# A four-layer graph network on one core: the three biases added by VectorE during the gathers, in place of TensorE's products at the layers' ends

## The chip, the core and the metric

The kernel runs on one NeuronCore of a Trainium2 chip. The metric is the device time of one execution in microseconds (us). Three runs of the kernel before took 8660.35, 8661.93 and 8672.08 us; their median, 8661.93 us, is its time.

## What is computed

Everything is float32. `x` has 12500 nodes of 32 features, and there are 200000 edges with a source, a destination, 32 attributes, a type of 86 and a weight; the edges come sorted by destination. Four layers follow, each with a residual:

```
h = relu(layernorm(x)); x = x + (h + segment_sum(relu(h[src] + edge_attr), dst)) @ W0.T + b0
h = relu(layernorm(x)); x = x + L1(h)
h = relu(layernorm(x)); x = x + relu(segment_sum(weight * h[src], dst) @ W2 + b2)
h = relu(layernorm(x)); x = x + segment_sum(h[src], dst) @ W3.T + b3
```

Layer 1 is a relational layer with 16 bases and attention. It adds, without a bias at its end, `relu(nei + curr)`, where `curr` is the row of one source (the node's last edge) times a self-loop weight.

## The kernel before

**Layout.** `x`, `h` and `t` lie in SBUF as 128 partitions x 98 blocks x 32 features, so 3136 columns. The sums over edges (`acc`) fill the first 3136 columns of PSUM: six banks of 512 columns and a seventh of which only 64 columns are used (BANKS = 7). The rest of PSUM's last bank holds small masks and, in its last 128 columns, `iota_ps`.

**A wide layer (0, 2 and 3).** The edges are cut into 1587 tiles of up to 128, four to a lot, so 397 lots: 49 rounds of eight (ROUNDS, RING) in a hardware loop and a remainder of five lots (REST) written out after it. For each lot POOL issues four gathers of 128 rows of the table of `h` in device memory (L511). It may run eight lots ahead of VectorE, whose buffers make the ring. VectorE makes one-hot matrices (L992) and spreads the gathered rows over four blocks of nodes (L1005 in layers 2 and 3; L1020, L1025 and L1030 in layer 0), and TensorE adds each tile to the sums (L1277). ScalarE copies the next indices (L586).

**A layer's end** is the time between the last gather of one layer and the first of the next. `linear` (L1305) goes over the seven banks. TensorE transposes the sums of a bank (L1300, four products with the identity), ScalarE copies them to SBUF (L613), and TensorE multiplies them by a block-diagonal weight (L1328, four products). The transposes of the next bank stand ahead of the products of this one in TensorE's queue. Ahead of the four products a fifth puts the bias into the bank: ones by `biasrow`, one partition deep and 512 columns wide (L1323), and the four accumulate on it. In layer 1, where there is no bias, a product of zeros stands there (L1320). In layers 2 and 3 ScalarE first copies the raw sums out of PSUM (L619); in layer 0 VectorE does that with `h` added (L1066).

**The residual and the norm.** VectorE runs `norm` in turns, one a bank, staggered: turn n holds the sum of squares of bank n-3 (L837), the centring of bank n-2 (L842), the sum of bank n-1 (L847) and then the residual of bank n (L1044, in layer 2 L1043, in layer 1 L1171), which waits for that bank's products. ScalarE squares each centred bank (L554). When all seven banks are through, a few short instructions on 98 columns (from L851 on) make the scale, seven more write `h` (L862), SP writes it to device memory, and POOL begins the next layer's gathers when all seven transfers have landed. After layer 3 there is no norm, and SP stores each bank of `x` when its residual is done (L443, the last one L445).

**Layer 1** first writes a table of products of all nodes. POOL meanwhile gathers 98 blocks of self-loop rows (L501), VectorE masks them (L1104) and `linear` with zeros follows. Then 104 rounds of 16 tiles run (STEPS_N / 16), with the gathers of POOL (L511 into `arena`), two long products of VectorE for each lot pair (L1138) and reductions (L1144). Its masks and coefficients overwrite `iota_ps`, which VectorE restores after the last round (L1167).

Of the kernel before, what the change touches and what calls it, by code (L numbers as in the profile page):

```python
# [82 lines left out]
def gnn(nc, x_in, src, dst, edge_attr, etype, weight, W0, b0, eps0, W1, wcomp, wself, A1, A1b, A2, A2b,  # L83
# [11 lines left out]
    with ctx:  # L95
# [5 lines left out]
        def sem(name):  # L101
            return ctx.enter_context(nc.semaphore(name))
# [53 lines left out]
        biasrow = sb("biasrow", [1, 3, D])  # L156
# [69 lines left out]
        iota_ps = ps[:, W7 + BANK - P:W7 + BANK]  # L226
        coef = ps[:, FEAT:FEAT + LOTS * HB * BASES].rearrange("p (h u b) -> p h u b", h=LOTS, u=HB)
# [40 lines left out]
        added = sem("residual_added")  # L268
        mean_ready = sem("mean_ready")
# [180 lines left out]
        def _(pool):  # L450
# [25 lines left out]
            for k, b in enumerate((b0, b2, b3)):  # L476
                pool.dma_start(biasrow[:, k, :], b.rearrange("(a f) -> a f", a=1)).then_inc(loaded, 16)
# [301 lines left out]
        def _(dve):  # L779
# [42 lines left out]
            def norm(l, residual):  # L822
# [9 lines left out]
                for turn in range(BANKS + 3):  # L832
                    b = turn - 3
# [100 lines left out]
            cp(wq[:, MSG + D:PROD], ps[:, W7 + 2 * P + D:W7 + 2 * P + 2 * D]).then_inc(wts_ready, 1)  # L934
# [72 lines left out]

            def wide_layer(l, body):

                with dve.Fori(0, ROUNDS) as i:  # L1010
                    body(i, RING)
                body(ROUNDS, REST)
# [24 lines left out]
            def linear_residual(q, relu):  # L1037

                def add(b):
                    w = columns(b)  # L1040
                    dve.wait_ge(lin_done, BANKS * q + b + 1)
                    if relu:
                        return nc.vector.scalar_tensor_tensor(xf[:, w], ps[:, w], 0.0, xf[:, w], ALU.max, ALU.add)  # L1043
                    return tt(xf[:, w], ps[:, w], xf[:, w], ALU.add)  # L1044
                return add

# [21 lines left out]
            norm(1, linear_residual(0, False))  # L1068
# [98 lines left out]
            step(cp(iota_ps, iota[:, :]))  # L1167
# [19 lines left out]
            norm(3, linear_residual(2, True))  # L1187
# [11 lines left out]
            last_add = linear_residual(3, False)  # L1199
# [5 lines left out]
        def _(pe):  # L1205
# [99 lines left out]
            def linear(q, w, bias):  # L1305

                for turn in range(BANKS + 1):
                    if turn < BANKS:
                        if bias is None:
                            pe.wait_ge(self_masked, turn + 1)  # L1310
                        else:
                            pe.wait_ge(t_ready, BANKS * (q if q < 2 else q - 1) + turn + 1)
                        transposes(selfrows.rearrange("p b f -> p (b f)") if bias is None else tf, turn)
# [3 lines left out]
                    n = min(BANK, FEAT - b * BANK)  # L1317
                    pe.wait_ge(hT_copied, BANKS * q + b + 1)
                    if bias is None:
# [14 lines left out]
            linear(0, 0, 0)  # L1334
# [31 lines left out]
            linear(1, 3, None)  # L1366
# [48 lines left out]
            linear(2, 1, 1)  # L1415
# [3 lines left out]
            linear(3, 2, 2)  # L1419
# [24 lines left out]
```

## Time and profile before

| | us |
|---|---|
| median of three runs | 8661.93 |
| lowest and highest | 8660.35, 8672.08 |
| the profiled execution, its own time | 8675.0 |
| its span in the profile | 8673.2 |
| busy: POOL | 6224.3 (72%) |
| busy: TensorE matmuls | 4674.7 (54%) |
| busy: VectorE | 4395.6 (51%) |
| busy: ScalarE | 2234.2 (26%) |

The profile records one execution. PE is TensorE's matmuls and PEld its weight loads, DVE is VectorE, ACT is ScalarE, POOL is GpSimd, SPq the queue that issues transfers. A line such as L1323 is a line of the kernel. TensorE's granted clock is given as a share of 2.4 GHz, so 0.50 is 1.2 GHz. Times of the timeline are us from the start of the span: start, duration, engine, line, operation; in brackets how long the engine had been idle before, and what ended that.

### The profile page before, as it was taken

The page shows a single profiled execution, that of the slowest core. Times are in us where ns is not written, and L with a number is a line of the kernel's source. Part 1 is how long each engine was busy: PE and PEld are TensorE (multiplying, and loading weights), DVE is VectorE, ACT ScalarE, POOL GpSimd, SP SyncE. Part 2 cuts the span into 40 slices and gives each one's busy share as a digit, 9 for nine tenths or more (in the row PEclk, how much of TensorE's full clock was granted, in tenths as well). Part 3 has the DMA queues.
Part 4 walks back from the last instruction along what each step waited for, and adds up shares of the span by engine and source line. Part 5 has one row for each costly group of instructions (what it writes and reads, how often), then busy time and mean ns, then how long its engine had stood idle before and what let it go on. Part 6 is the DMA issues. An engine that isn't in the chain of part 4 may idle for free. (4 is left out here: it accounts for less than half of the span.)

```text
span 8673.2 us, 104883 instructions
## 1 busy us (share of the span) xinstructions
PE 4674.7 (54%) x23835; PEld 4127.8 (48%) x23836; DVE 4395.6 (51%) x8833; ACT 2234.2 (26%) x5812; POOL 6224.3 (72%) x6577
## 2 busy tenths in 40 slices
PE   4555555555777777777774444444445444444444
PEld 3444444444677777777773333333333333333333
DVE  6555555555688888888884222222223222222222
ACT  1000000002688788888881000000000000000000
POOL 6777777776666666666665777777775777777776
PEclk6555555556555555555555555555555555555555
DMA  4111111113788888888881000000000000000001
GB/s 84 26 26 26 26 26 26 26 26 97 232 245 245 244 246 243 246 244 246 245 243 34 13 13 13 13 13 13 13 13 18 13 13 13 13 13 13 13 13 18
DMA packets 599594, 726.39 MB, mean 84 GB/s; under 512 B 339548, under 2 KB 433308, under 8 KB 596385
## 3 DMA queue, kind: packets, MB, share of 16 engines
q0 software_dynamic: 290064, 544.60, 24.1%
q1 hardware_dynamic: 309497, 181.39, 7.6%
q8 instruction: 16, 0.26, 0.0%
q14 instruction: 17, 0.14, 0.0%
HBM read 685.53 MB, written 40.64 MB: 84 GB/s over the span
## 5 line engine op out<-in xcount | busy, mean ns | idle before, releaser
L511 POOL DMA_INDIRECT lanes<-table,idx x4764 | 4522.7, 949 | 1546.7 <-issue 1451.4
L1277 PE MATMUL ps<-arena 128*128 128x128 f32 x9528 | 2718.5, 458 | 3232.5 <-DVE arena L1005 2337.4
L1277 PEld LDWEIGHTS ps<-arena 128*128 128x128 f32 x9528 | 2267.9, 328 | 3644.8 <-issue 3570.0
L511 POOL DMA_INDIRECT arena<-table,idx x1664 | 1581.3, 950 | 756.7 <-issue 485.1
L1005 DVE TENSOR_TENSOR arena<-lanes,ps 128x512 f32<-128x512 f32 x794 | 545.7, 687 | 2858.5 <-DMA lanes<-table,idx 2858.5
L586 ACT COPY idx<-tabs 128x4 int32 (+1 forms) x1191 | 228.3, 193 | 5727.9 <-DMA lanes<-table,idx 5723.1
L992 DVE TENSOR_TENSOR arena<-ps,node 128x512 f32<-128x512 f32 (+1 forms) x1588 | 1048.3, 680 | 0.0
L1269 PE MATMUL ps<-lanes 128*128 128x32 f32 x3328 | 752.2, 402 | 485.1 <-issue 281.4
L1269 PEld LDWEIGHTS ps<-lanes 128*128 128x128 f32 x3328 | 725.4, 330 | 511.8 <-issue 511.8
L1377 PE MATMUL ps<-t,arena 128*128 x3328 | 955.0, 402 | 0.0
L1377 PEld LDWEIGHTS ps<-t,arena 128*128 128x128 f32 x3328 | 860.3, 318 | 0.1
L1375 PEld LDWEIGHTS ps<-relparts,arena 128*128 128x128 bf16 x4992 | 593.9, 171 | 167.9 <-ACT arena L710 156.9
L1020 DVE TENSOR_TENSOR lanes<-lanes 128x128 f32<-128x128 f32 x397 | 118.8, 299 | 980.6 <-DMA lanes<-table,idx 971.6
L1375 PE MATMUL ps<-relparts,arena 128*128 128x48 bf16 x4992 | 510.3, 219 | 140.2 <-ACT arena L710 140.2
L743 ACT ACTIVATE arena<-iota,tabs 128x128 f32<-128x128 f32 x1664 | 531.6, 392 | 0.0
L1138 DVE TENSOR_TENSOR arena<-arena,ps 128x2048 f32<-128x2048 f32 x208 | 475.6, 2286 | 7.1
L1138 DVE TENSOR_TENSOR tT<-arena,ps 128x2048 f32<-128x2048 f32 x208 | 474.1, 2279 | 0.0
L1144 DVE TENSOR_REDUCE lanes<-tT 128x128 f32<-128x2048 f32 x208 | 473.3, 2275 | 0.0
L1144 DVE TENSOR_REDUCE lanes<-arena 128x128 f32<-128x2048 f32 x208 | 473.3, 2275 | 0.0
L722 ACT ACTIVATE arena<-arena,part 128x1024 f32<-128x1024 bf16 x416 | 472.5, 1136 | 0.3
L1030 DVE SCALAR_TENSOR_TENSOR arena<-lanes,ps 128x128 f32<-128x128 f32 x1588 | 344.5, 277 | 0.0
L1280 PE MATMUL ps<-lastrow,arena 128*128 128x8 bf16 x1588 | 339.8, 214 | 0.0
(201 smaller groups left out, 2908.9 us busy)
## 6 DMA issues: line engine op xcount, KB each, us to landing
arena<-step_rows SPq DMA_DIRECT2D x416, 256.0 KB, 4.6
lanes<-table,idx POOLq DMA_INDIRECT x4764, 2.4
arena<-table,idx POOLq DMA_INDIRECT x1664, 4.1
table<-arena SPq DMA_DIRECT2D x24, 1088.0 KB, 6.0
lanes<-in_edge_attr SPq DMA_DIRECT2D x384, 64.0 KB
table<-h SPq DMA_DIRECT2D x18, 256.0 KB, 2.4
edge_rows<-arena SPq DMA_DIRECT2D x1, 2496.0 KB, 8.4
lanes<-self_loop_table,selfi POOLq DMA_INDIRECT x98, 2.4
```

The lines of the kernel that those rows point to most:

```text
L511: pool.indirect_dma_start(out=into, out_offset=None, in_=tableD[l], in_offset=bass.IndirectOffsetOnAxis(ap=index, axis=0)).then_inc(there, 16)
L722: nc.scalar.activation(off[:, :, :, :], rowb[:, k], ACT.Abs, scale=-1.0, bias=part[:, 0:1]).then_inc(off_ready[k], 1)
L743: last = nc.scalar.activation(away[:, u, :], iota[:, :], ACT.Abs, scale=-1.0, bias=tabs[:, DLOC, bass.ds(i * BODY + (k * HB + u), 1)])
L992: tt(to[:, k], iota_ps.unsqueeze(1).to_broadcast([P, HB, P]), node[:, bass.ds(i * ROUND + (EXN + k * HB), HB)].unsqueeze(2).to_broadcast([ ...
L1005: tt(wmsg[:, k], rows_[:, k].unsqueeze(2).to_broadcast([P, HB, WB, D]), factors[:, k].unsqueeze(3).to_broadcast([P, HB, WB, D]), ALU.mult) ...
L1030: last = nc.vector.scalar_tensor_tensor(wmsg[:, k, u], total[:, k % LOTS, u].unsqueeze(1).to_broadcast([P, WB, D]), 0.0, mask[:, k, u].uns ...
L1138: tt(prods[k % 2][:, :, :, :], g1[:, k, :, 0:MSG].rearrange("p u (o b) -> p u o b", o=D), coef[:, k].unsqueeze(2).to_broadcast([P, HB, D, ...
L1144: nc.vector.reduce_sum(msg[:, k], prods[k % 2][:, :, :, :], AX.X).then_inc(msg_ready[k], 1)
L1269: last = mm(ps[:, bass.ds(w[u], D)], onehot[:, k, u, :], msg[:, k, u], start=False, stop=True, skip_group_check=True)
L1277: last = mm(ps[:, bass.ds(w[u], WB * D)], onehotw[:, k, u, :], wmsg[:, k, u].rearrange("p w f -> p (w f)"), start=False, stop=True, skip_g ...
L1375: mm(ps7[:, u, :], relT[:, k, u, :], relparts[:, part_, :], start=(part_ == 0), stop=False, skip_group_check=True)
L1377: last = mm(ps7[:, u, BASES:YC], nodeT[:, k, u, :], yf[:, bass.ds(w[u], D)], start=False, stop=True, skip_group_check=True)
```

## The change

VectorE adds the bias to `x` in one instruction of 3136 columns between the hardware loop and the five last lots of a wide layer, while POOL gathers. The operand that is repeated over the 98 blocks is `bias_ps`, 96 columns of PSUM that VectorE fills in the prologue and again after layer 1. In layer 2 the bias stands inside the relu, so there the sum goes to `h`, which is free by then: `h = x + b2`. At the end `h` takes up the products, and `x` becomes the larger of `h` and `x`, because x + relu(y) = max(x + y, x). Thus a bank takes two instructions there, and the first of them stands at the head of its turn. TensorE no longer multiplies ones or zeros; the first of the four products of a bank opens the accumulation itself. The bias vectors are loaded into all 128 partitions.

```diff
@@ buffers
-        biasrow = sb("biasrow", [1, 3, D])
+        biasrow = sb("biasrow", [P, 3, D])
+        bias_ps = ps[:, W7 + BANK - P - 3 * D:W7 + BANK - P].rearrange("p (k f) -> p k f", k=3)
+        summed = sem("sums_and_bias_added")
@@ POOL, prologue
-                pool.dma_start(biasrow[:, k, :], b.rearrange("(a f) -> a f", a=1)).then_inc(loaded, 16)
+                pool.dma_start(biasrow[:, k, :], b.partition_broadcast(P)).then_inc(loaded, 16)
@@ VectorE, norm
-            def norm(l, residual):
+            def norm(l, residual, sums=None):
...
                 for turn in range(BANKS + 3):
+                    if sums and turn < BANKS:
+                        sums(turn).then_inc(summed, 1)
@@ VectorE, prologue
-            cp(wq[:, MSG + D:PROD], ps[:, W7 + 2 * P + D:W7 + 2 * P + 2 * D]).then_inc(wts_ready, 1)
+            step(cp(wq[:, MSG + D:PROD], ps[:, W7 + 2 * P + D:W7 + 2 * P + 2 * D]))
+            cp(bias_ps, biasrow[:, :, :]).then_inc(wts_ready, 1)
@@ VectorE, wide layers
+            def add_bias(to, k):
+
+                step(tt(to[:, :, :], x[:, :, :], bias_ps[:, k].unsqueeze(1).to_broadcast([P, BLOCKS, D]), ALU.add))
+
             def wide_layer(l, body):
 
                 with dve.Fori(0, ROUNDS) as i:
                     body(i, RING)
+                if l == 2:
+                    dve.wait_ge(table_out[2], BANKS * 16)
+                add_bias(h if l == 2 else x, TURN[l])
                 body(ROUNDS, REST)
@@ VectorE, residuals
-            def linear_residual(q, relu):
+            def linear_residual(q):
...
-                    if relu:
-                        return nc.vector.scalar_tensor_tensor(xf[:, w], ps[:, w], 0.0, xf[:, w], ALU.max, ALU.add)
                     return tt(xf[:, w], ps[:, w], xf[:, w], ALU.add)
...
+            def sums_of_2(b):
+
+                w = columns(b)
+                dve.wait_ge(lin_done, BANKS * 2 + b + 1)
+                return tt(hf[:, w], ps[:, w], hf[:, w], ALU.add)
+
+            def relu_residual(b):
+
+                w = columns(b)
+                dve.wait_ge(summed, b + 1)
+                return tt(xf[:, w], hf[:, w], xf[:, w], ALU.max)
@@ VectorE, end of layer 1
-            step(cp(iota_ps, iota[:, :]))
+            cp(iota_ps, iota[:, :])
+            step(cp(bias_ps, biasrow[:, :, :]))
@@ VectorE, end of layer 2
-            norm(3, linear_residual(2, True))
+            norm(3, relu_residual, sums_of_2)
@@ TensorE, linear
-                    if bias is None:
-                        mm(ps[:, b * BANK:(b + 1) * BANK], zeros[0:1, 0:P], zeros[0:1, :], start=True, stop=False,
-                           skip_group_check=True)
-                    else:
-                        mm(ps[:, b * BANK:b * BANK + n], ones[0:1, :],
-                           biasrow[:, bias, :].unsqueeze(1).to_broadcast([1, n // D, D]), start=True, stop=False,
-                           skip_group_check=True)
...
                         last = mm(ps[:, g * P:g * P + m], tT[0:m, g * P:(g + 1) * P], wdiag[0:m, w, 0:m],
-                                  start=False, stop=True, skip_group_check=True)
+                                  start=(g == 4 * b), stop=True, skip_group_check=True)
```

## Rows read from the trace of the kernel before

**Rows 1.** Groups by line: busy us, mean ns of one, idle before and its releasers.

```profile
L511 POOL DMA_INDIRECT lanes<-table,idx x4764 | 4522.7, 949 | 1546.7 <-issue 1451.4 <-DMA table<-h 95.3
...
L511 POOL DMA_INDIRECT arena<-table,idx x1664 | 1581.3, 950 | 756.7 <-issue 485.1 <-DVE arena L1138 270.1 <-DVE tT L1138 1.5
```

**Rows 2.** Timeline of the end of layer 3.

```profile
8639.09 1.97 PE L1300 MATMUL ps<-ident,t 128*128 128x128 f32 x8 [0.75 <-ACT t L619]
...
8640.99 2.07 PE L1323 MATMUL ps<-biasrow,ones 1*128 1x512 f32 x2
...
8642.99 2.08 PE L1328 MATMUL ps<-wdiag,tT 128*128 128x128 f32 x8
...
8645.85 2.07 PE L1323 MATMUL ps<-biasrow,ones 1*128 1x512 f32 x2
...
8668.66 0.69 PE L1323 MATMUL ps<-biasrow,ones 1*128 1x64 f32 x2
...
8670.00 0.23 DVE L1044 TENSOR_TENSOR x<-ps,x 128x64 f32<-128x64 f32 x1 [0.54 <-PE ps L1328]
```

**Rows 3.** Stretches: window, length, busy by engine, granted PE clock, DMA share, GB/s.

```profile
8650.00:8660.00 10.00, 10.00 (x31) 6.33 (x30) 1.66 (x3) 1.77 (x4) 0.00 (x0) 0.50 0.33 52
2077.80:2078.40 0.60, 0.60 (x2) 0.00 (x0) 0.06 (x1) 0.09 (x1) 0.00 (x0) 0.88 0.00 0
6627.80:6628.40 0.60, 0.60 (x3) 0.30 (x2) 0.60 (x2) 0.54 (x1) 0.00 (x0) 0.91 0.00 0
```

**Rows 4.** Timeline of the end of layer 0.

```profile
2070.44 1.97 PE L1300 MATMUL ps<-ident,t 128*128 128x128 f32 x8 [1.68 <-DVE t L1066]
...
2076.45 0.69 DVE L1044 TENSOR_TENSOR x<-ps,x 128x512 f32<-128x512 f32 x1 [2.59 <-PE ps L1328]
...
2082.70 1.12 PE L1323 MATMUL ps<-biasrow,ones 1*128 1x512 f32 x2
...
2085.28 1.12 PE L1323 MATMUL ps<-biasrow,ones 1*128 1x512 f32 x2
...
2095.86 0.21 DVE L851 TENSOR_SCALAR small<-small 128x98 f32<-128x98 f32 x1
```

**Rows 5.** Timeline of the end of layer 1.

```profile
4589.22 0.29 DVE L1167 COPY ps<-iota 128x128 f32<-128x128 f32 x1 [3.67 <-PE ps L1269]
4589.55 0.69 DVE L1171 SCALAR_TENSOR_TENSOR x<-ps,x 128x512 f32<-128x512 f32 x1
...
4605.76 0.21 DVE L851 TENSOR_SCALAR small<-small 128x98 f32<-128x98 f32 x1
```

**Rows 6.** Timeline of the end of layer 2.

```profile
6606.41 1.97 PE L1300 MATMUL ps<-ident,t 128*128 128x128 f32 x8 [0.68 <-ACT t L619]
...
6612.43 0.69 DVE L1043 SCALAR_TENSOR_TENSOR x<-ps,x 128x512 f32<-128x512 f32 x1 [8.89 <-PE ps L1328]
...
6639.02 0.21 DVE L851 TENSOR_SCALAR small<-small 128x98 f32<-128x98 f32 x1
```

**Rows 7.** Timeline of the start of layer 1's rounds.

```profile
2232.61 0.23 DVE L1104 TENSOR_TENSOR lanes<-lanes,has_edge 128x64 f32<-128x64 f32 x1 [3.20 <-DMA lanes<-self_loop_table,selfi]
...
2234.84 0.26 ACT L613 COPY tT<-ps 64x128 f32<-64x128 f32 x1 [3.63 <-PE ps L1300]
```

**Rows 8.** Groups by line, VectorE's long product in layer 1.

```profile
L1138 DVE TENSOR_TENSOR arena<-arena,ps 128x2048 f32<-128x2048 f32 x208 | 475.6, 2286 | 7.1
```

**Rows 9.** Timeline of VectorE in the first of layer 0's five last lots.

```profile
2042.21 0.29 DVE L1020 TENSOR_TENSOR lanes<-lanes 128x128 f32<-128x128 f32 x1 [2.56 <-DMA lanes<-table,idx]
```

**Rows 10.** Groups by line in the stretch 65 to 78 us.

```profile
L511 POOL DMA_INDIRECT lanes<-table,idx x8 | 12.5, 1564 | 2.4 <-issue 2.4
...
L966 DVE TENSOR_SCALAR arena<-arena 128x1697 int32<-128x1697 int32 x1 | 1.1, 1120 | 0.0
```

**Rows 11.** Stretches of layer 1, VectorE's line L1138 alone, eleven of 200 us.

```profile
3100.00:3300.00 200.00, 78.13 (x35) 0.50 0.81 243
...
sum 2200.00, DVE 876.51; mean DVE 79.68
```

More of the change, by code:

```diff
@@ L226, in gnn @@
         iota_ps = ps[:, W7 + BANK - P:W7 + BANK]
+        bias_ps = ps[:, W7 + BANK - P - 3 * D:W7 + BANK - P].rearrange("p (k f) -> p k f", k=3)
+        assert 2 * ROUND * WB + 3 * D + P <= BANK
         coef = ps[:, FEAT:FEAT + LOTS * HB * BASES].rearrange("p (h u b) -> p h u b", h=LOTS, u=HB)
@@ L1067, in _ @@
                                                ).then_inc(t_ready, 1)
-            norm(1, linear_residual(0, False))
+            norm(1, linear_residual(0))
             yf = y[:, :, :].rearrange("p b f -> p (b f)")
@@ L1198, in _ @@
             wide_layer(3, body3)
-            last_add = linear_residual(3, False)
+            last_add = linear_residual(3)
             for b in range(BANKS):
@@ L1303, in _, with linear @@
             tf, hf = (v[:, :, :].rearrange("p b f -> p (b f)") for v in (t, h))
-            def linear(q, w, bias):
+            def linear(q, w, of_self):
                 for turn in range(BANKS + 1):
                     if turn < BANKS:
-                        if bias is None:
+                        if of_self:
                             pe.wait_ge(self_masked, turn + 1)
@@ L1312, in linear @@
                             pe.wait_ge(t_ready, BANKS * (q if q < 2 else q - 1) + turn + 1)
-                        transposes(selfrows.rearrange("p b f -> p (b f)") if bias is None else tf, turn)
+                        transposes(selfrows.rearrange("p b f -> p (b f)") if of_self else tf, turn)
                     b = turn - 1
@@ L1316, in linear @@
                         continue
-                    n = min(BANK, FEAT - b * BANK)
                     pe.wait_ge(hT_copied, BANKS * q + b + 1)
-                    if bias is None:
-                        mm(ps[:, b * BANK:(b + 1) * BANK], zeros[0:1, 0:P], zeros[0:1, :], start=True, stop=False,
-                           skip_group_check=True)
-                    else:
-                        mm(ps[:, b * BANK:b * BANK + n], ones[0:1, :],
-                           biasrow[:, bias, :].unsqueeze(1).to_broadcast([1, n // D, D]), start=True, stop=False,
-                           skip_group_check=True)
                     for g in range(4 * b, min(4 * b + 4, GROUPS)):
@@ L1333, in _ @@
             scatters(0)
-            linear(0, 0, 0)
+            linear(0, 0, False)
             def transpose_parts(g):
@@ L1365, in _ @@
             pe.wait_ge(p1_biased, BLOCKS)
-            linear(1, 3, None)
+            linear(1, 3, True)
             def edge_terms(i, k, w, n):
@@ L1414, in _ @@
             scatters(2)
-            linear(2, 1, 1)
+            linear(2, 1, False)
             pe.wait_ge(added, 4 * BANKS)
@@ L1418, in _ @@
             scatters(3)
-            linear(3, 2, 2)
+            linear(3, 2, False)
 _INS = ['x', 'src', 'dst', 'edge_attr_32', 'edge_type_86', 'edge_weight', 'L0_gnn_W', 'L0_gnn_b', 'L0_gnn_eps',
```

## The prediction

> **What bounds the kernel now.** I read the page's busy times first, then the groups by line, then the timeline of the ends, because the change touches little else. In the wide layers POOL is the bound. A gather takes 0.95 us and 0.30 us of issue (1451.4 / 4764) follow, so one starts every 1.25 us, and POOL's idle time before these gathers has no other entry but 95.3 us in which it waited for a table [rows 1]. Work of VectorE in those stretches costs nothing as long as it fits; work taken out of a layer's end, where POOL stands still, counts in full. In layer 1 POOL waits 270.1 us for VectorE's products, so its rounds are a circle of VectorE, POOL and transfers.
>
> In layer 3's end TensorE is the bound: it is busy for 10.00 of 10.00 us [rows 3]. A bank there takes 8645.85 - 8640.99 = 4.86 us, of which the bias product is 8642.99 - 8640.99 = 2.00 us [rows 2]. These are rows at a granted clock of 0.50, the lower level. In layer 0's end the clock rose at about 2077.9 us [rows 3], some 7.4 us after the first transposes, and from there on a bank takes 2085.28 - 2082.70 = 2.58 us, with 1.1 us of bias in it [rows 4].
>
> VectorE sets the floor of the other ends. Layer 1's end has no products to wait for: from the first residual to the scale it takes 4605.76 - 4589.55 = 16.2 us [rows 5]. Four instructions of a full bank start some 0.6 us apart, so a turn is 2.4 us. The same stretch takes 2095.86 - 2076.45 = 19.4 us in layer 0 [rows 4] and 6639.02 - 6612.43 = 26.6 us in layer 2 [rows 6].
>
> **The change, part by part.** All is measured against the profiled execution, 8675.0 us; the median of the runs is 13.1 us below it, and I carry the difference over unchanged.
>
> *Clock of the new ends.* Without the bias a bank costs TensorE 4.86 - 2.00 = 2.86 us at the lower level and 2.58 - 1.1 = 1.5 us at the upper. Which level is granted no row can show, since no end before was free of these products. What the engine did before each of the two rises was the same: four products and four transposes without a break, the last things ahead of a bias product. In layer 3's end each such stretch is broken by a one-partition product after 2.9 us, and the clock stayed at 0.50 for 30 us although TensorE was never idle [rows 2, 3]. In the new ends nothing breaks the stretch. So I take the clock to rise in each of them as late as it did in layer 0, 7.4 us after the first transposes, and hold both extremes for the range.
>
> The Trainium skill (TensorE: Matmul & The Clock Gate, Part 1) says that the throttled level is the default and that sustained activity releases it. Taken for busy time alone this disagrees with the trace, where an always busy TensorE was left at 1.2 GHz; for the new ends it would give the upper level, as I forecast.
>
> *Layer 0's end.* The first residual comes 2.0 us earlier, at 2074.45. If it never waited, the scale would follow 16.2 us later, at 2090.7: 5.2 us gained. But VectorE is ready for the second residual 1.3 us after the first (0.7 + 0.6), and the second bank's products come 2.86 us after the first's, at the lower clock: a wait of 1.55 us. The third is then ready about in time. **3.7 us** gained. At the lower level throughout, further waits of 1.06 us (2.86 - 1.8) and three of 0.46 us (2.86 - 2.4) leave 1.2 us. Ends: 1.2 and 5.2 us.
>
> *Layer 1's start.* The zero products go too. POOL's self-loop gathers hide most of them, but the transposes of the last bank stood behind one. Their input is ready at 2232.61 + 0.23 = 2232.84, and ScalarE's copy starts at 2234.84 [rows 7]; with 0.5 us for the few transposes of the narrow bank (eight take 1.97 us [rows 2]) it can start at 2233.4. ScalarE makes the first selectors right behind that copy, and the rounds start with these. **1.4 us** gained. It carries through, if the circle keeps its rhythm; between 0 and 1.5 us.
>
> *Layer 1's end.* One more copy, 96 columns behind 128. The first with its wait takes 4589.55 - 4589.22 = 0.33 us [rows 5], and the second overlaps it in part: **0.2 us lost** (0.1 to 0.33).
>
> *Layer 2's end.* Again the first products come 2.0 us earlier, at 6610.4. VectorE has 16.2 us of norm as in layer 1 and now seven sums on top, 6 x 0.6 + 0.3 = 3.9 us, so 20.1 us and the scale at 6630.5 instead of 6639.02: 8.5 us. A wait of 1.55 us before the second sum leaves **6.9 us**; at the lower level throughout, waits of 1.06 and 0.5 us more leave 5.3 us. From the fourth bank on a turn of five instructions (3.0 us) is longer than a bank of TensorE at either level (2.86 us), so VectorE becomes the bound here. That the sum stands at the head of its turn, ahead of three instructions of the norm, costs nothing in that case, because it doesn't wait.
>
> *Layer 3's end.* From 8639.09 to 8670.00 are 30.9 us [rows 2]. Six bias products of 2.00 us and the narrow one (0.69 us at most) go: 12.7 us, if the clock stays low. If it rises after 7.4 us, 18.2 - 7.4 = 10.8 us of lower-level work are left and shrink by 1.5 / 2.86 to 5.7 us: 4.9 us more, 17.6 in all. VectorE has one 0.7 us instruction a bank, and ScalarE two copies; both fit. The stores are next: at 0.33 of the transfer engines over 10 us, or two banks, one bank's store takes 1.6 us [rows 3], a little more than the 1.5 us in which banks now come. I take off 0.6 us: **17.0 us**. Ends: 12.7 and 18.6.
>
> *The adds under the gathers.* The nearest row is VectorE's product of 2048 columns with an operand in PSUM, 2.29 us [rows 8]; 3136 columns are 3.5 us. Between lots VectorE is idle for 2.56 us even in layer 0 [rows 9], so the first of the five last lots is 0.9 us late and the second has caught up; layers 2 and 3 have more room. POOL may run eight lots ahead and sees nothing. Gone is that cover only if the add stops POOL itself, a rival below. **0**.
>
> *The prologue.* A copy and a wait on VectorE (0.3 us) and three slightly larger loads of POOL's queue. VectorE's first lot waits for other data anyway, and POOL waits for a transfer behind its loads. **0**, at most 0.3 us lost.
>
> Sum: 3.7 + 1.4 - 0.2 + 6.9 + 17.0 = 28.8 us. 8675.0 becomes 8646.2, and the median 8661.9 - 28.8 = **8633 us**. Of the sum, 8 to 9 us rest on the clock.
>
> **Rivals.** A measurement of this kernel tells a change of 0.2% (17.3 us) from none: below 8644.6 us is faster, above 8679.3 slower.
>
> *The clock stays low in the new ends.* For it speaks that it did so for 30 us in layer 3; against it, that what kept the stretches short is what is removed. Then 1.2 + 1.4 - 0.2 + 5.3 + 12.7 = 20.4 us: 8641.5 us. Chance 0.22.
>
> *The adds stop POOL.* In the prologue eight gathers took 1564 ns each while VectorE ran integer instructions of 1697 columns at about 0.6 ns a column [rows 10], against 949 ns [rows 1]. So VectorE can hold up a gather, by about its own duration. Three adds of 3.5 us would cost 10.5 us: 8643.6 us. Against it: the 2286 ns products of layer 1 are of the add's kind, one operand in PSUM and about 1.1 ns a column, and the gathers beside them keep 950 ns [rows 1, 8]. Chance 0.06.
>
> The Trainium skill (GPSIMD Engine Reference, section 8, Key points) names contention with instructions in a two-port mode or with two inputs in SBUF. By that the add, with one input in PSUM, is free, and the sum would stay as it is.
>
> *Slower: the rounds of layer 1 settle into another rhythm.* They start with transfers, VectorE and POOL offset otherwise. In the slices of 200 us VectorE's products hold 78.13 us in the poorest and 79.68 us in the mean [rows 11]; poorest throughout would be 1.9% of the 2357 us between the last mask and the copy at the end (2232.61 to 4589.22 [rows 5, 7]), 45 us longer: 8678 us. It decides from 0.28 us a round on (28.8 / 104), below which the kernel is still faster. Against it: the slices differ by no more than the products that an edge cuts off, over 2000 us, so the circle looks stable. Chance 0.04.
>
> *The circle absorbs the early start* or small waits take as much: up to 5 us less than forecast, 8638 us; it is inside the forecast's own range.
>
> **How the numbers follow.** The forecast, with the clock up in some or all of the ends, has 0.65; its own range is 8627 (all upper ends, 34 us, and a little) to 8638. The rivals hold 0.32, and 0.03 is left for what I don't see. The range reaches down to 8623, since the runs before differ by up to 12 us and their median may stand some us off, and up to 8646, which takes in the low clock and stopped gathers. Faster: 0.65, most of the low clock's 0.22 and half of the stopped gathers' 0.06, together 0.86. Slower by over 0.2%: 0.03. Within: 0.11.
>
> **What would show it.** In the profile after: no L1323 or L1320 groups; a bank of layer 3's end 2.9 us and later 1.5 us long, with a granted clock of 1.00 before the last banks; layer 2's end with VectorE without a gap from the fourth turn on and the scale 20 to 22 us after the first sum; three adds of 3.4 to 3.5 us with gathers of 0.95 us beside them; the first selector distances 1.4 us sooner after the last mask. It is wrong if the granted clock stays at 0.50 in all ends, if a gather beside an add is longer, or if the stretch of layer 1's rounds changes by more than 2 us.

## The result and the profile after

On the chip of the prediction's runs the changed kernel takes 8642.41 us (median of 9 runs, 8637.83 to 8646.37). The kernel before takes 8668.71 us there (median of 9, 8660.35 to 8673.08). The ratio is 0.997, 95% interval [0.9962, 0.9978], so the change saves 26.3 us (19 to 33 us).

The two profiled executions are 34.0 us apart: 8675.0 and 8640.96 us, spans 8673.2 and 8639.1 us. The profiled run of before lies 6.3 us above its median and the one of after 1.5 us below; 34.0 - 6.3 - 1.5 = 26.2 us, which is what the medians say. The ledger below is of the profiles and so adds up to 34 us; some 8 us of that belong to these two executions and not to the change, and in which rows they lie one profile of each kernel can't show.

Groups of instructions of the kernel after, by line (busy us, mean ns of one, idle before and its releasers). L514 is the gather, L1344 the products and L1324 the transposes of `linear`; before they were L511, L1328 and L1300.

```profile
L514 POOL DMA_INDIRECT lanes<-table,idx x4764 | 4522.6, 949 | 1538.4 <-issue 1450.3 <-DMA table<-h 86.9 <-DVE lanes L1033 0.9
...
L514 POOL DMA_INDIRECT arena<-table,idx x1664 | 1581.1, 950 | 753.8 <-issue 486.0 <-DVE arena L1161 266.8 <-DVE tT L1161 0.9
...
L1344 PE MATMUL ps<-wdiag,tT 128*128 128x128 f32 (+1 forms) x200 | 34.4, 325 | 6.3 <-ACT tT L616 6.1
```

Beside [rows 1] the gathers and their issue are unchanged, and POOL waits 8.4 us less for tables. Those 8.4 us are not all of the gain, since the idle time before the first gather into `arena` and the end after the last gather don't count there. The groups of the bias products and of `linear`'s zero products are gone.

**Layer 0's end.** Timeline of after (start, duration, engine, line, idle before):

```profile
2070.44 1.97 PE L1324 MATMUL ps<-ident,t 128*128 128x128 f32 x8 [1.68 <-DVE t L1089]
...
2074.32 1.06 PE L1344 MATMUL ps<-wdiag,tT 128*128 128x128 f32 x8
...
2075.65 1.06 PE L1344 MATMUL ps<-wdiag,tT 128*128 128x128 f32 x8
```
VectorE in the same end:

```profile
2074.09 0.69 DVE L1055 TENSOR_TENSOR x<-ps,x 128x512 f32<-128x512 f32 x1 [0.22 <-PE ps L1344]
...
2075.41 0.69 DVE L1055 TENSOR_TENSOR x<-ps,x 128x512 f32<-128x512 f32 x1
...
2090.31 0.21 DVE L856 TENSOR_SCALAR small<-small 128x98 f32<-128x98 f32 x1
```

Four products and four transposes take 1.33 us (2075.65 - 2074.32) from the second bank on, and the second residual doesn't wait. Beside [rows 4] the first residual is 2.36 us earlier and the scale 5.55 us.

The granted clock of the three ends stands in the stretches of after (window, length, busy by engine, granted clock, DMA share, GB/s). Layer 0's end:

```profile
2073.00:2074.50 1.50, 1.50 (x13) 1.50 (x12) 1.28 (x4) 0.03 (x1) 0.00 (x0) 0.79 0.04 11
2074.50:2076.00 1.50, 1.50 (x16) 1.50 (x16) 1.47 (x3) 0.73 (x2) 0.00 (x0) 1.00 0.00 0
```
Layer 2's end:

```profile
6603.00:6604.00 1.00, 1.00 (x10) 1.00 (x9) 0.97 (x2) 0.54 (x2) 0.00 (x0) 0.94 0.00 0
```
Layer 3's end:

```profile
8627.00:8628.00 1.00, 1.00 (x10) 1.00 (x9) 0.57 (x1) 0.43 (x1) 0.00 (x0) 0.88 0.00 0
8628.00:8630.00 2.00, 2.00 (x20) 2.00 (x20) 0.90 (x2) 1.72 (x4) 0.00 (x0) 1.00 0.83 131
8630.00:8633.00 3.00, 3.00 (x29) 3.00 (x28) 1.72 (x3) 1.55 (x4) 0.00 (x0) 1.00 1.18 183
8633.00:8636.00 3.00, 0.78 (x6) 0.52 (x5) 0.96 (x3) 0.00 (x0) 0.00 (x0) 1.00 1.60 177
```

The clock rises 3.2, 4.3 and 4.3 us after the first transposes of the ends of layers 0, 2 and 3. In the kernel before it rose 7.5 us and 21.5 us after them in layers 0 and 2, and not at all in layer 3's [rows 2, 3].

**Layer 2's end**, VectorE's timeline of after; L1062 adds the products to `h`, L1068 is the new residual:

```profile
6602.76 0.69 DVE L1062 TENSOR_TENSOR h<-ps,h 128x512 f32<-128x512 f32 x1 [6.78 <-PE ps L1344]
6603.48 0.69 DVE L1068 TENSOR_TENSOR x<-h,x 128x512 f32<-128x512 f32 x1
6604.35 0.69 DVE L1062 TENSOR_TENSOR h<-ps,h 128x512 f32<-128x512 f32 x1 [0.17 <-PE ps L1344]
...
6611.53 0.68 DVE L1062 TENSOR_TENSOR h<-ps,h 128x512 f32<-128x512 f32 x1
...
6614.52 0.69 DVE L1062 TENSOR_TENSOR h<-ps,h 128x512 f32<-128x512 f32 x1
...
6622.98 0.21 DVE L856 TENSOR_SCALAR small<-small 128x98 f32<-128x98 f32 x1
```

A turn is 2.99 us, five instructions, and the only wait for products is 0.17 us. From the first sum to the scale are 20.2 us, where before 26.6 us went by [rows 6]. VectorE is the bound.

**Layer 3's end**, timeline of after; L446 and L448 issue the stores:

```profile
8622.97 1.97 PE L1324 MATMUL ps<-ident,t 128*128 128x128 f32 x8 [0.75 <-ACT t L622]
...
8627.60 8.85 SPq L446 DMA_DIRECT2D out_nodes<-x  x7
...
8628.70 1.06 PE L1344 MATMUL ps<-wdiag,tT 128*128 128x128 f32 x8
...
8630.03 1.06 PE L1344 MATMUL ps<-wdiag,tT 128*128 128x128 f32 x8
...
8633.45 0.82 DVE L1055 TENSOR_TENSOR x<-ps,x 128x512 f32<-128x512 f32 x2 [0.31 <-PE ps L1344]
8636.49 0.42 SPq L448 DMA_DIRECT2D out_nodes<-x  x1
```

A bank takes 1.33 us in place of 4.86 us [rows 2]. The residuals are through at 8634.27, but the last store is issued at 8636.49: the stores run at 131 to 183 GB/s, against 52 in the row of before [rows 3], and end last. (Their DMA share of 1.60 adds up transfers that are under way at the same time, so it can pass 1.)

**Layer 1**, timeline of its start in after:

```profile
2227.06 0.23 DVE L1127 TENSOR_TENSOR lanes<-lanes,has_edge 128x64 f32<-128x64 f32 x1 [1.85 <-DMA lanes<-self_loop_table,selfi]
...
2228.34 0.26 ACT L616 COPY tT<-ps 64x128 f32<-64x128 f32 x1 [1.33 <-PE ps L1324]
```
And of its end:

```profile
4581.30 0.29 DVE L1190 COPY ps<-iota 128x128 f32<-128x128 f32 x1 [3.70 <-PE ps L1293]
4581.51 0.25 DVE L1191 COPY ps<-biasrow 128x96 f32<-128x96 f32 x1
...
4598.00 0.21 DVE L856 TENSOR_SCALAR small<-small 128x98 f32<-128x98 f32 x1
```

The ledger, forecast beside measured:

| stretch | forecast us gained | measured |
|---|---|---|
| up to layer 0's end, adds and prologue | 0 | 0.0 |
| layer 0's end | 3.7 | 5.55 |
| layer 1's start (last mask to copy: 2.23, now 1.28) | 1.4 | 0.95 |
| layer 1's rounds (copy to copy: 2354.38, now 2352.96) | 0 | 1.4 |
| layer 1's end | -0.2 | -0.2 |
| wide loops of layers 2 and 3 | 0 | -0.1 |
| layer 2's end | 6.9 | 8.5 |
| layer 3's end | 17.0 | 17.9 |
| sum | 28.8 | 34.0 |

### The profile page after: what moved, and what is told of

Read it like the earlier page. It is cut to its first block and busy times, and to the rows that moved or that the text cites. A ratio compares the mean times of both kernels' runs of the same rounds, so it can differ in the third digit from the quotient of the medians.

```text
span 8639.1 us, 104786 instructions
## 1 busy us (share of the span) xinstructions
PE 4614.4 (53%) x23779; PEld 4105.4 (48%) x23780; DVE 4408.8 (51%) x8845; ACT 2233.6 (26%) x5812; POOL 6224.5 (72%) x6577
## 5 line engine op out<-in xcount | busy, mean ns | idle before, releaser
L514 POOL DMA_INDIRECT lanes<-table,idx x4764 | 4522.6, 949 | 1538.4 <-issue 1450.3
L514 POOL DMA_INDIRECT arena<-table,idx x1664 | 1581.1, 950 | 753.8 <-issue 486.0
```

What stands on the lines that cost most here:

```text
L514: pool.indirect_dma_start(out=into, out_offset=None, in_=tableD[l], in_offset=bass.IndirectOffsetOnAxis(ap=index, axis=0)).then_inc(there, 16)
```

## Experiments

Two causes were to be told apart: what made the clock rise (the missing one-partition products, or chance), and whether the adds and VectorE's new instructions cost what the sum says. The twelve runs fell on three other chips, A, B and C. There the kernel before takes 10295 to 10404 us, most of it because its wide loops are slower. The groups of 1000 us of layer 3 in the kernel before, on the first chip:

```profile
L511 POOL DMA_INDIRECT lanes<-table,idx x801 | 757.2, 945 | 244.2 <-issue 244.2
```
The same on chip C (before_b):

```profile
L511 POOL DMA_INDIRECT lanes<-table,idx x692 | 653.2, 944 | 356.6 <-issue 205.3 <-DVE arena L1005 149.4 <-ACT idx L586 1.9
...
L987 DVE TENSOR_TENSOR ps<-ps,tabs 128x16 f32<-128x16 f32 x179 | 31.7, 177 | 756.3 <-remote 657.2 <-issue 94.1 <-PE ps L1277 4.5
```

A gather is as long, but POOL now waits for VectorE, and VectorE for something that the profile doesn't name. The mean granted clock over these 1000 us is 0.58, against 0.50 on the first chip. What makes these chips slower stays open. The ends of the layers, where the change works, are made of the same instructions with the same durations, so kernels are compared by their ends and by ratios on one chip. Two kernels that are the same up to layer 0's end (after_again and l3zero_b) reach it 8.5 us apart there, and layer 1's rounds, which are the same in all four kernels on chip B, take 2908.4 to 2915.0 us in their profiles. So medians tell less than the ends do.

The ends of all profiles in us, from the timelines and the record of the granted clock: when the clock rises after the first transposes of layer 0's end; layers 0's and 2's ends from the first transposes to the scale; layer 3's to the end of the span.

| kernel, chip | clock rises | layer 0 | layer 2 | layer 3 | ratio to before, 95% |
|---|---|---|---|---|---|
| before, first | 7.5 | 25.4 | 32.6 | 34.1 | |
| after, first | 3.2 | 19.9 | 24.1 | 16.2 | 0.997 [0.9962, 0.9978] |
| before_again, A | 12.4 | 27.7 | 22.2 | 21.5 | |
| deep, A | 4.1 | 22.4 | 20.9 | 18.4 | 0.9989 [0.9981, 0.9998] |
| l3zero, A | 4.6 | 20.5 | 22.5 | 23.7 | 0.9982 [0.9973, 0.999] |
| onesum, A | 4.0 | 20.3 | 18.8 | 14.8 | 0.9967 [0.9955, 0.9979] |
| after_again, B | 5.4 | 20.9 | 22.5 | 14.8 | 0.9978 [0.9969, 0.9987] |
| l3zero_b, B | 5.8 | 21.1 | 22.5 | 21.2 | 0.9984 [0.9975, 0.9993] |
| threeadds, B | 4.5 | 20.5 | 22.5 | 14.8 | 0.9985 [0.9976, 0.9993] |
| poolboth, B | 3.6 | 22.4 | 23.1 | 14.8 | 0.9986 [0.9977, 0.9995] |
| before_b, C | 21.7 | 32.6 | 22.2 | 20.6 | |
| deep_b, C | 4.3 | 22.5 | 20.9 | 18.4 | 0.9979 [0.997, 0.9988] |
| allzero, C | 16.7 | 29.8 | 25.8 | 29.2 | 0.9998 [0.999, 1.0007] |
| pooladd, C | 4.4 | 20.5 | 21.8 | 14.8 | 0.9981 [0.9972, 0.9989] |

### The kernel before, twice

No edit.

> The kernel before, unchanged, for a second profile of it. The runs of before lie between 8660 and 8673 us. If the place at which the granted clock rises in the layers' ends makes that spread, the two profiles differ in the lengths of the ends (layer 2's 26.6 us from the first residual to the scale, layer 3's 30.9 us from the first transposes to the last residual) and agree elsewhere to 1 us. The rival, that the rounds of layer 1 or the gathers make it, has the ends equal to 0.5 us and another stretch longer or shorter by several.

> The kernel before once more: when the granted clock rises in its layers' ends. If its one-partition products keep the clock low, it rises 7 us or more after the first transposes of layer 0's end, as in the profile of before (7.4 us) and on the second kind of chip (12.5 us), where the changed kernel and the others without such products had 3.2 to 5.8 us. Rival (the moment is chance): anywhere between 3 and 13 us.

Measured: 10398.98 and 10289.78 us. Stretches of layer 0's end in before_b:

```profile
2421.00:2436.00 15.00, 15.00 (x46) 9.50 (x45) 6.01 (x10) 2.92 (x5) 0.00 (x0) 0.50 0.00 0
2436.00:2440.50 4.50, 4.50 (x20) 2.46 (x19) 3.82 (x7) 1.48 (x3) 0.00 (x0) 0.88 0.00 0
```
And nearly all of layer 3's:

```profile
10267.40:10282.00 14.60, 14.41 (x77) 9.00 (x77) 3.46 (x5) 6.16 (x13) 0.00 (x0) 1.00 0.46 73
```

The clock rose 12.4 and 21.7 us after the first transposes in layer 0's end, later than the 7.5 us of the first chip, and until then TensorE was busy without a gap. That is before_b's theory (7 us or more); its rival, 3 to 13 us by chance, is passed by far. What before_again was to find, where the first chip's spread of 13 us comes from, stays open, because it ran on another chip. In the ends of layers 2 and 3 the clock was already up when they began, since 4.8 to 7.2 us before the first transposes: there a bank takes 2.58 us, and the ends are 10 and 13 us shorter than on the first chip. So the clock's part of the gain differs from chip to chip.

### Bias products 128 partitions deep

The kernel before, with the same number of products of the same columns:

```diff
-                        mm(ps[:, b * BANK:b * BANK + n], ones[0:1, :],
-                           biasrow[:, bias, :].unsqueeze(1).to_broadcast([1, n // D, D]), start=True, stop=False,
+                        mm(ps[:, b * BANK:b * BANK + n], deep[:, :],
+                           biasrow[:, bias, :].unsqueeze(1).to_broadcast([P, n // D, D]), start=True, stop=False,
```

`deep` holds 1/128 everywhere and `biasrow` the bias in each partition.

> The kernel before with its bias products 128 partitions deep instead of one: weights of 1/128 everywhere and the bias vector in all partitions, so the same 512 columns and the same sums. My theory, that one-partition products kept the clock down: the clock rises within 4 to 8 us of an end's first transposes; layer 3's end shrinks from 30.9 to about 20 us, layer 2's from 26.6 to about 18, layer 0's by 1 to 3, in all 17 to 23 us less than before. The rival, that the clock follows the amount of TensorE's work or chance and not the depth of these products: granted clock 0.50 through layer 3's end as before, and a time within 4 us of before.

> The kernel before with its bias products 128 partitions deep (all ones/128 against the bias in all 128 partitions): as many products, columns and cycles as before. Theory (it is the one-partition form that keeps the clock low): the clock rises within 6 us of the first transposes in layer 0's end, and on a chip where before's layer 3 stays at 0.50 it rises there too, so that this end takes some 20 us in place of 30.9 and the kernel is 10 us or more faster than before. Rival (form is of no account): rise and ends as in the kernel before, time within 4 us of it.

Measured: 10392.24 us (11.4 us less than before) and 10279.41 us (16.0 us less). TensorE in layer 0's end of deep_b:

```profile
2416.32 1.97 PE L1302 MATMUL ps<-ident,t 128*128 128x128 f32 x8 [1.68 <-DVE t L1068]
2418.12 2.07 PE L1325 MATMUL ps<-biasrow,deep 128*128 128x512 f32 x2
...
2421.60 1.02 PE L1325 MATMUL ps<-biasrow,deep 128*128 128x512 f32 x2
2422.46 1.05 PE L1330 MATMUL ps<-wdiag,tT 128*128 128x128 f32 x8
```

A stretch of it:

```profile
2420.60:2421.40 0.80, 0.80 (x10) 0.80 (x9) 0.04 (x1) 0.00 (x0) 0.00 (x0) 1.00 0.00 0
```

At the lower level the deep product has the flat one's 2.07 us [rows 2], and yet the clock rises after 4.1 and 4.3 us in place of 12.4 and 21.7. Order, number and columns of TensorE's instructions are those of before; what differs is the depth of one in five, with the values that go with it, and a little of its time: from its start to the next row it takes 1.86 us (2419.98 - 2418.12) where the flat one takes 2.00 [rows 2]. So it is the one-partition form that keeps the clock low. Whether by its depth or by a short pause beside it that the records don't show, of which the 0.14 us may be a sign, stays open. As to the times, deep's forecast of 17 to 23 us less than before missed, with 11.4, and deep_b's of 10 us or more was met, with 16.0. Both had counted on ends of layers 2 and 3 that stay at the lower level, and on these chips they don't. The ends of layers 2 and 3 are 1.3 and 2 to 3 us shorter too, although the clock was up in both kernels: from its start to the next row a deep product takes 0.86 us at the upper level (2422.46 - 2421.60), a flat one 1.05 us in before_b.

### One-partition products of zeros put back

The changed kernel, for the end of layer 3 alone (l3zero, l3zero_b) or for those of layers 0, 2 and 3 (allzero, `q != 1`):

```diff
+                    if q == 3:
+                        n = min(BANK, FEAT - b * BANK)
+                        mm(ps[:, b * BANK:b * BANK + n], zeros[0:1, 0:P], zeros[0:1, 0:n], start=True, stop=False,
+                           skip_group_check=True)
...
-                                  start=(g == 4 * b), stop=True, skip_group_check=True)
+                                  start=(q != 3 and g == 4 * b), stop=True, skip_group_check=True)
```

> The changed kernel with one product of zeros, one partition deep, put back ahead of the four of each bank in layer 3's end alone, as wide as the bias product was. My theory: the clock stays at 0.50 for most of that end and its banks take about 4.9 us again, so 17 to 19 us more than the changed kernel. The rival, that the clock now rises anyway and only the products' own time counts: banks of 2.4 to 2.6 us, the clock at 1.00 after some 5 us, and 6 to 9 us more.

> The changed kernel with one one-partition product a bank (its left operand zero) ahead of the products of layer 3's end alone. Theory (broken stretches keep the clock low): on a chip on which the kernel before shows a granted clock of 0.50 all through layer 3's end, this end is again at 0.50 and as long as before, 30.9 us from the first transposes to the last residual, so that 16 to 19 us of the change's gain are gone and 8 to 15 are left. Rival (the clock rises with busy time, whatever the form of the products): it rises here some 4 us after the first transposes as in the changed kernel, the products added cost 1.1 us a bank, and the end is about 8 us longer than the changed kernel's, 22 us in all.

> The changed kernel with a one-partition product of zeros ahead of each bank's products in the ends of layers 0, 2 and 3: TensorE's work is as before, the rest is the changed kernel's. Theory (broken stretches keep the clock low): in layer 0's end the clock rises 7 us or more after the first transposes, and that end's gain (5 to 7 us) is gone; in layer 3's end 2.0 us a bank are back at the lower clock, 1.05 us at the upper; in layer 2's end VectorE is the bound at either level, so it is lengthened by no more than its first two banks. In all 14 to 24 us slower than the changed kernel, no faster than before by more than 10 us. Rival (the clock rises as in the changed kernel, 3 to 6 us after the transposes): the ends of layers 0 and 3 are 4 and 8 us longer, 12 us in all.

Measured: 10386.57, 10282.75 and 10297.12 us. Stretches of allzero in layer 0's end:

```profile
2426.00:2436.00 10.00, 10.00 (x31) 6.22 (x29) 3.54 (x6) 1.70 (x3) 0.00 (x0) 0.50 0.00 0
2436.50:2441.00 4.50, 4.50 (x25) 2.78 (x25) 3.88 (x7) 2.14 (x4) 0.00 (x0) 1.00 0.00 0
```
And in layer 3's end of allzero:

```profile
10267.30:10270.00 2.70, 2.52 (x13) 1.45 (x14) 0.00 (x0) 2.44 (x5) 0.00 (x0) 1.00 0.00 0
10270.00:10287.00 17.00, 17.00 (x55) 11.17 (x54) 2.77 (x4) 3.01 (x8) 0.00 (x0) 0.50 0.29 46
10287.00:10290.00 3.00, 3.00 (x13) 1.51 (x13) 0.69 (x1) 0.71 (x2) 0.00 (x0) 0.98 0.56 87
```
The low stretch of l3zero in the same end:

```profile
10357.30:10364.00 6.70, 6.70 (x24) 4.54 (x23) 1.38 (x2) 1.07 (x2) 0.00 (x0) 0.50 0.25 39
```
And l3zero_b's end, in two stretches:

```profile
10255.60:10270.60 15.00, 14.81 (x79) 9.09 (x78) 3.46 (x5) 5.94 (x13) 0.00 (x0) 1.00 0.44 70
10270.70:10273.00 2.30, 2.30 (x11) 1.96 (x9) 0.69 (x1) 0.00 (x0) 0.00 (x0) 0.50 0.72 114
```

With allzero the whole gain is gone: 0.9998 of before, and by the ratios, each of which is good to some 9 us, 20 us more than the changed kernel on its chip. In layer 0's end the clock rises late again, 16.7 us after the first transposes, and in layer 3's it even falls from the upper level and stays at 0.50 for 17 us while TensorE is never idle. The same happened in l3zero for 6.8 us, but in l3zero_b only 15.3 us after the first transposes, so that there the product cost little more than its own 1.05 us a bank: 21.2 against 14.8 us. Falls of the clock under a TensorE that had been busy without a gap for 13 us or more occur in five profiles, one each in the three of before, in l3zero_b and in allzero (23.3 us after the first transposes), and each time in an end with one-partition products. In the ends without them the clock fell only where TensorE had gaps. (The early falls, 2.8 us into the end in allzero and 2.9 in l3zero, come after 0.75 and 0.18 us in which TensorE waited.) So one-partition products can hold the clock down, and these profiles suggest that they let it fall, too; when it happens varies from run to run.

The forecasts: allzero's theory holds in the time (14 to 24 us) and in layer 0's end. For layer 3 alone the theory missed: l3zero's end is 8.9 us longer than onesum's on the same chip, not 17 to 19, and l3zero_b's 6.4 us longer than after_again's, near the rivals' 6 to 9 and 8 us. An end of 30.9 us, as on the first chip, came in neither run. Here the end began with the clock up, so the chip that l3zero_b's theory asks for was not met. Layer 2's end is 25.8 us in allzero, 3.6 us longer than in before: with the clock up and the products still there, VectorE's second instruction a bank is a pure cost.

The Trainium skill (TensorE: Matmul & The Clock Gate, Part 1) has the gate follow how busy TensorE has been. The row of 15.00 busy us in 15.00 at 0.50 shows that the busy time of the records is not enough; the measurement decides.

### One instruction a bank in layer 2

The changed kernel with the fused residual of before in layer 2. Nothing adds b2, so this output lacks it.

```diff
-            norm(3, relu_residual, sums_of_2)
+            def one_residual(b):
+
+                w = columns(b)
+                dve.wait_ge(lin_done, BANKS * 2 + b + 1)
+                return nc.vector.scalar_tensor_tensor(xf[:, w], ps[:, w], 0.0, xf[:, w], ALU.max, ALU.add)
+
+            norm(3, one_residual)
```

> The changed kernel, but layer 2's end has one instruction a bank again (the larger of products and zero, added to x); the bias of layer 2 is left out of the result, while its add under the gathers still runs. My theory, that VectorE bounds this end at both levels: the seven sums are gone and the stretch from the first of VectorE's residuals to the scale falls from 20.2 to 16.2 to 16.8 us, 3.5 to 4 us less in all. The rival, that TensorE or ScalarE's copies and squares come next: under 1.5 us less.

Measured: 10372.45 us, 0.9967 of before. Layer 2's end is 18.8 us against 22.5 us in l3zero on the same chip: 3.7 us for six sums of a full bank and a narrow one, which is the prediction's 3.9 us. The other ends are the changed kernel's.

### The changed kernel, and three wide adds in place of one

```diff
-                add_bias(h if l == 2 else x, TURN[l])
+                to = h if l == 2 else x
+                add_bias(to, TURN[l])
+                for op in (ALU.subtract, ALU.add):
+                    step(tt(to[:, :, :], to[:, :, :], bias_ps[:, TURN[l]].unsqueeze(1).to_broadcast([P, BLOCKS, D]), op))
```

> The changed kernel once more, beside the kernel before on the same chip. If the gain is made in the layers' ends, it is 26 to 34 us here too, whatever this chip's wide loops take: first residual to scale 16 to 17 us in layer 0's end, 20 to 21 us from the first sum to the scale in layer 2's, and 11 to 17 us from the first to the last instruction of layer 3's end. If part of the gain came from the wide loops or from layer 1's rounds, it is another number here, or these stretches differ between the two kernels by more than 2 us.

> The changed kernel, with a subtract and another add behind each of its three adds of 3136 columns: nine such instructions in place of three. Forecast of the prediction (they lie under the gathers and cost nothing): 0 to 1 us slower than the changed kernel; in the profile each is 3.4 us, the lot behind them 7 us late, and the gathers beside them stay at 0.95 us. Rival (a two-operand add stops POOL for its own duration): six more of 3.4 us are 20 us slower, and gathers of 1.5 us or more beside them.

Measured: 10273.94 and 10279.80 us. The medians are 5.9 us apart, less than the 8.5 us by which equal kernels differ before layer 0's end. POOL in layer 3 of threeadds:

```profile
10226.28 0.95 POOL L514 DMA_INDIRECT lanes<-table,idx  x1 [0.30 <-issue]
```

The four gathers behind it are of 0.94 and 0.95 us.
VectorE at the same time, the three adds:

```profile
10226.78 3.41 DVE L1016 TENSOR_TENSOR x<-x,ps 128x3136 f32<-128x3136 f32 x1
10230.23 6.88 DVE L1027 TENSOR_TENSOR x<-x,ps 128x3136 f32<-128x3136 f32 x2
```

No gather beside any of the adds is longer than 0.95 us. In after on the first chip four gathers ran beside each of the three adds; in threeadds gathers ran beside five of the nine. All three ends of threeadds are the changed kernel's within 0.4 us. The rival of 20 us has fallen; up to some us in the medians can't be told from the noise of these chips.

The changed kernel saves 22.4 us here (13 to 32). Its forecast of 26 to 34 missed by the median; its three lengths, 17.0, 20.0 and 14.8 us, are as expected. The gain is close to the 26 of the first chip, but made up otherwise. Against the profiles of before on chips A and C, for chip B has none, it is about 7 to 12 us in layer 0's end, where before's clock rises so late, nothing in layer 2's (22.5 against 22.2), and 6 to 7 us in layer 3's. The rest, 4 to 10 us, was not traced; layer 1's rounds alone differ by 6.6 us between kernels that are equal there, so it may be no more than noise. Whether all of the gain lies in the ends is shown on the first chip alone.

### Work of VectorE handed to POOL

pooladd hands over the addition of layer 2's branch, poolboth also the centring of norms 1 to 3:

```diff
+                            pool.tensor_tensor(out=x[:, w, :], in0=h[:, w, :], in1=x[:, w, :], op=ALU.add
+                                               ).then_inc(added, 1)
...
+                            pool.tensor_tensor(out=h[:, w, :], in0=x[:, w, :],
+                                               in1=small[:, 0, w].unsqueeze(2).to_broadcast([P, w.stop - w.start, D]),
+                                               op=ALU.subtract).then_inc(centered, 1)
...
-                add_bias(h if l == 2 else x, TURN[l])
+                add_bias(x, TURN[l])
...
-                return tt(hf[:, w], ps[:, w], hf[:, w], ALU.add)
+                return tt(h[:, w, :], ps[:, columns(b)].rearrange("p (b f) -> p b f", f=D),
+                          negrow[:, :].unsqueeze(1).to_broadcast([P, w.stop - w.start, D]), ALU.max)
```

> The changed kernel with VectorE relieved at the ends of layers 0 to 2, where it is the bound: POOL, idle there, does the centring of norms 1 to 3 and in layer 2 the addition of the branch to x (x takes b2 under the gathers; VectorE takes the larger of products and -b2 from PSUM). VectorE's turn falls from four instructions of a full bank to three and a small one, in layer 2 from five to three and a small one. Theory (VectorE bounds these ends at 0.6 us an instruction and bank): the ends of layers 1 and 2 shrink by 3 and 6 us if POOL's instruction over 1024 columns takes no more than 1.8 us, the end of layer 0 by at most 2, 8 to 11 us in all against the changed kernel. Rival (POOL is slower per column, 2.4 us or more, and its two instructions a bank in layer 2 become the bound): 0 to 10 us slower.

> The changed kernel with only the addition of layer 2's branch handed to POOL (x takes b2 under the gathers, VectorE takes the larger of products and -b2 from PSUM into h, POOL adds h to x; in the run before POOL took 1.26 us a bank for it), while the centring stays with VectorE. Theory (VectorE bounds layer 2's end, 0.6 us an instruction and bank): a turn falls from five instructions to four, and the end from the first sum to the scale from 20.0 us to 16.5 to 17.5: 3 us faster than the changed kernel, the only change. Rival (what POOL takes comes back as waits of VectorE between banks, as it did with the centring): 0 to 2 us.

Measured: 10286.64 us (0.9986) and 10273.19 us (0.9981); neither is faster than the changed kernel (0.9978). In poolboth the ends of layers 0 to 2 are 22.4, 18.6 (first residual to scale, 16.2 before) and 23.1 us. Both theories missed (8 to 11 us and 3 us faster than the changed kernel). In poolboth POOL is quick enough, with 1.05 us for a centring against the 1.8 us that the theory allowed, but the square of a bank now waits for a round trip VectorE, POOL, ScalarE. POOL of poolboth in layer 1's end:

```profile
5571.55 1.05 POOL L561 TENSOR_TENSOR h<-x,small 128x512 f32<-128x512 f32 x1 [1.54 <-DVE small L869]
```
And VectorE:

```profile
5570.70 0.69 DVE L861 TENSOR_REDUCE small<-t 128x16 f32<-128x512 f32 x1 [0.64 <-ACT t L576]
...
5573.29 0.69 DVE L861 TENSOR_REDUCE small<-t 128x16 f32<-128x512 f32 x1 [0.64 <-ACT t L576]
```

A turn is 2.59 us (5573.29 - 5570.70) with a wait of 0.64 us in each, longer than the 2.4 us of four instructions. In the full turns of pooladd no such wait appears, and still the end shrinks by 0.7 us only, the rival's 0 to 2 us but not by its mechanism. VectorE's timeline of layer 2's end there:

```profile
7928.93 0.68 DVE L860 TENSOR_REDUCE small<-t 128x16 f32<-128x512 f32 x1
7929.53 1.38 DVE L865 SCALAR_TENSOR_TENSOR h<-small,x 128x512 f32<-128x512 f32 x1
```

The centring (L865) takes 1.38 us in place of 0.68 in the turns in which POOL adds beside it, and a turn is 3.1 us although it holds four instructions. Reductions and the `max` with an operand in PSUM keep 0.68 us. The Trainium skill (SBUF — State Buffer, Who interferes with whom) says that a VectorE instruction with two inputs in SBUF contends with a POOL instruction that reads SBUF. The row agrees.

## Why the prediction was right

**The frame held.** POOL's gathers and the wide loops did not move (0.0 and -0.1 us), and in the profiles the gain lies at the layers' ends and at layer 1's start, but for 1.4 us in layer 1's rounds. Of the level's miss, 8642.4 against 8633, 6.8 us are not of the change: the median of three runs, 8661.9, lay that far below the median of nine. The gain itself was forecast as 28.8 and measured as 26.3 us by the medians and 34.0 by the profiles. By its time alone the result does not speak for the forecast: 8642.4 lies above the forecast's own range (8627 to 8638) and next to the low-clock rival's 8641.5. It is inside the stated range because that was drawn wide for this rival and for the base, and that 28.8 comes so near to 26.3 is in part luck: the parts were forecast for the profiled executions, and there they add up to 34.0. What tells the two apart is the granted clock in the profile.

**The clock of the new ends** rises in each of them, as taken, and the rival of a low clock (20.4 us) is out. The reason given was that one-partition products break the stretches. The two deep runs and allzero bear out that these products are the cause, in layer 0's end, the only one that begins at the lower level on those chips. Whether it is because they break stretches, as the prediction had it, they don't show; only that the one-partition form decides and not the order or the number of products. Mis-sized was the moment: 3.2 and 4.3 us after the first transposes in place of 7.4, because 7.4 was read from an end that still had the products. In the ten profiles without them in layer 0's end the rise comes after 3.2 to 5.8 us, in the four with them after 7.5 to 21.7.

**Layer 0's end**, 3.7 against 5.55, above the upper bound of 5.2. The second bank's products came early enough, so the wait of 1.55 us did not arise, and the first residual came 2.36 us earlier in place of 2.0 because the clock rose within the first bank's products. From the first residual to the scale are 16.22 us, the floor read from layer 1.

**Layer 1's start**, 1.4 against 0.95. The step that failed took the last transposes to be free at 2232.84. They still stand behind the previous bank's four products, so that they start 0.8 us after the last mask. **Its end**, 0.2, was right; the copy's own 0.25 us overlap in part.

**Layer 2's end**, 6.9 against 8.5. VectorE's 20.1 us were measured as 20.2; only the wait of 1.55 us before the second sum was too much (0.17). onesum prices the sums at 3.7 us.

**Layer 3's end**, 17.0 against 17.9. With the rise at 4.3 us the prediction's own formula gives 18.2 - 4.3 = 13.9 us of work that shrinks by 1.5 / 2.86, which saves 6.6 us, and 12.7 + 6.6 = 19.3; measured to the last residual 19.8. The stores take back 1.9 us (from the last residual's start to the end 3.2 before, 5.1 now) in place of 0.6.

**Adds under the gathers**: 3.41 us each, gathers of 0.95 beside them, cost 0. **The rhythm of layer 1's rounds**: 1.4 us shorter; the prediction had nothing for it, and why is open.

## What to carry to other kernels

Work taken from an engine counts where that engine ends the wait, so price each end by the engine that bounds it at the clock that is granted there: on the chips where TensorE was already at the upper level, layer 2's end gained nothing. A TensorE product one partition deep can cost more than its own time, because it can keep the clock low for everything around it. Where it can't be dropped, try it 128 partitions deep, which took 5 to 10 us off layer 0's end here (22.4 and 22.5 against 27.7 and 32.6); depths in between were not measured. An operation handed to POOL is not free for VectorE if both read two operands from SBUF (1.38 against 0.68 us), and it can add a round trip.

## What was not expected

TensorE without a gap stayed at 1.2 GHz for 21.7 us in layer 0's end of before_b and for 17 us in allzero, there after it had been at 2.4 GHz, and the clock rose within 5.8 us in each end that began at 1.2 GHz and had no one-partition products. A VectorE instruction of 512 columns with two SBUF inputs went from 0.68 to 1.38 us beside an addition of POOL. And three chips run this kernel 19 to 20% slower than the first (10295 to 10404 against 8669 us) with gathers of nearly the same length (944 to 949 ns).

Two things were not tried: the deep form in layer 2 alone (20.9 us there against the changed kernel's 22.5 with the clock up), with the adds elsewhere; and deep or allzero on a chip where layer 3 of before stays at the lower level.
